# Linear attention: mask added in PSUM by TensorE, scores taken out half by ScalarE, half by VectorE; cross-attention clamp with a floor tile

## What is computed

```python
qp = relu(einsum('bhtd,hdm->bhtm', q_ch, proj))      # 64 features
kp = relu(einsum('bhtd,hdm->bhtm', k_ch, proj))
aw = einsum('bhtm,bhsm->bhts', qp, kp) * mask        # mask = tril(ones(128, 128))
out = (ctx_hist + aw @ v) / (norm_hist + aw.sum(-1) + 1e-6)
```

## Time and profile before

| | busy us | share of the span |
|---|---|---|
| TensorE matmul (PE) | 1311.8 | 89% |
| TensorE weight load (PEld) | 1113.5 | 76% |
| VectorE (DVE) | 911.7 | 62% |
| ScalarE (ACT) | 573.1 | 39% |
| GpSimd (POOL) | 795.9 | 54% |

### The profile page before, as it was taken

One profiled execution on the slowest core, in us unless ns is written; L12 is line 12 of the kernel. 1 busy time (PEld: TensorE's weight loads), 2 busy tenths in 40 slices (PEclk: granted clock), 3 DMA queues, 4 the chain that ended last, 5 costly groups with the idle time before them and its releaser, 6 DMA issues.

```text
span 1473.3 us, 23156 instructions
## 1 busy us (share of the span) xinstructions
PE 1311.8 (89%) x9073; PEld 1113.5 (76%) x9073; DVE 911.7 (62%) x1729; ACT 573.1 (39%) x1172; POOL 795.9 (54%) x761
## 2 busy tenths in 40 slices
PE   6998999999999999988899888987884699999980
PEld 6997788888888888866666666666653699999980
DVE  4656622632442262234687787777884699999966
ACT  3566311211121121124344444433342477777742
POOL 4444566666576576523232344535565347888831
PEclk9998999999999999999899999988885799999995
DMA  5101233233343233213324324235531755666605
GB/s 177 39 18 39 73 99 122 86 101 101 107 136 100 86 100 100 75 42 83 108 64 121 94 68 111 52 110 134 144 144 36 227 203 209 231 234 227 223 15 165
DMA packets 63101, 169.53 MB, mean 115 GB/s; under 512 B 11029, under 2 KB 30735, under 8 KB 55056
## 3 DMA queue, kind: packets, MB, share of 16 engines
q1 hardware_dynamic: 52432, 122.19, 27.8%
q0 software_dynamic: 10560, 45.86, 8.8%
HBM read 138.57 MB, written 33.38 MB: 117 GB/s over the span
## 4 chain that ended last, share of the span: by engine, by line
PE 71%; DVE 16%; ACT 3%; issue 3%; POOL 2%; DMA 2%; SPq 1%; ACTq 0%; POOLq 0%; DVEq 0%
PE bank L410 16%; PE bank L412 15%; PE bank L411 15%; PE bank L1297 9%; PE bank L418 4%; PE bank L1056 3%; PE bank L1137 3%; DVE topE L1809 3%; DVE shiftE L1816 3%; DVE topE L1811 1%; PE bank L1213 1%; ACT x_tok L458 1%; PE bank L1124 1%; PE bank L1192 1%; DVE x_tok L1977 1%
## 5 line engine op out<-in xcount | busy, mean ns | idle before, releaser
L1680 DVE CAST hid_hi<-bank 128x512 fp32r<-128x512 f32 x96 | 66.4, 691 | 252.1 <-ACT bank L1412 251.0
L552 POOL TENSOR_TENSOR wpiece_lo<-wraw,wpiece_hi 128x1024 fp32r<-128x1024 f32 x88 | 211.1, 2398 | 7.3
L410 PE MATMUL bank<-hid_hi,wpiece_lo 128*128 128x512 f32 x512 | 199.3, 389 | 0.0
L412 PE MATMUL bank<-hid_hi,wpiece_hi 128*128 128x512 f32 x512 | 199.2, 389 | 0.0
L411 PE MATMUL bank<-hid_lo,wpiece_hi 128*128 128x512 f32 x512 | 199.2, 389 | 0.0
L550 POOL TENSOR_SCALAR wpiece_hi<-wraw 128x1024 fp32r<-128x1024 f32 x88 | 94.1, 1069 | 154.7 <-PE bank L412 126.7
L1412 ACT ACTIVATE bank<-bank,ffn_scales 128x512 f32<-128x512 f32 x64 | 42.4, 662 | 301.5 <-PE bank L412 301.5
L1498 ACT ACTIVATE staging<-bank 128x512 f32<-128x512 f32 x128 | 70.0, 599 | 129.4 <-PE bank L1213 117.7
L412 PEld LDWEIGHTS bank<-hid_hi,wpiece_hi 128*128 128x128 f32 x512 | 96.1, 188 | 20.1
L410 PEld LDWEIGHTS bank<-hid_hi,wpiece_lo 128*128 128x128 f32 x512 | 96.1, 188 | 20.1
L411 PEld LDWEIGHTS bank<-hid_lo,wpiece_hi 128*128 128x128 f32 x512 | 96.1, 188 | 20.0
(11 more groups left out here) (342 smaller groups left out, 3696.9 us busy)
## 6 DMA issues: line engine op xcount, KB each, us to landing
wraw<-in_C_w SPq DMA_DIRECT2D x88, 512.0 KB, 3.6
w2raw<-in_F_w SPq DMA_DIRECT2D x8, 1152.0 KB, 7.2
w1raw<-in_F_w SPq DMA_DIRECT2D x8, 1028.0 KB, 7.4
split_qk<-qk_hi SPq DMA_DIRECT2D x64, 128.0 KB, 3.8
xt_lo<-split_qk SPq DMA_DIRECT2D x8, 1024.0 KB, 6.4
xt_hi<-split_qk SPq DMA_DIRECT2D x8, 1024.0 KB, 5.1
split_qk<-qk_lo SPq DMA_DIRECT2D x32, 128.0 KB
split_qk<-ctx_raw SPq DMA_DIRECT2D x32, 128.0 KB, 3.8
```

Source lines behind the costliest of these rows:

```text
L410: pe.e.matmul(o, sl, mh, start=start and i == 0, stop=False)
L412: made = pe.e.matmul(o, sh, mh, start=False, stop=stop and i == n - 1)
L552: pool.e.tensor_tensor(pair[1], raw, f(pair[0]), ALU.subtract).then_inc(done, 1)
```

## The change

TensorE: ahead of the score matmuls of a D pair, two matmuls (one for each head) of an identity with a tile of two copies of the transposed mask, 0 or -2**126, put the mask into the two diagonal blocks; the score matmuls then add to it (`start=False`). These operands are in the type float32r. `mask_d` now holds mask, mask and identity. The wait for `s_mask` goes ahead of it.

The step that takes scores out is then a maximum with 0: for QUAD step 1 on VectorE (`tensor_scalar` in the place of `tensor_tensor`), for QUAD step 2 on ScalarE (Relu).

The load of `mask_d` moves: it goes to `aw[0]`, once C's last result has been taken out, and GpSimd copies it from there to `mask_d` ahead of its D and E steps. The waits on `l_db` count one load less.

The clamp of E's maxima (L1811) becomes a `scalar_tensor_tensor` with the tile `floor_e` (-lim, filled once by GpSimd) in the place of the second constant.

```diff
+MASK_ON_ACT, MASK_ON_DVE = (2,), (1,)
@@ GpSimd
+            pool.e.memset(floor_e[:, :], -lim).then_inc(s_vone, 1)
+            pool.wait_ge(l_ffn, 48)
+            pool.e.tensor_scalar(mask_d[:, :], aw[0][:, 0, :], 1.0, 0.0, ALU.mult, ALU.add).then_inc(s_mask, 1)
             for name, step, args in DE:
@@ SyncE
-            load(mask_d[:, :], a["mask_d"], l_db)
             load(dbo[:, :], a["D_bo"], l_db)
             last = use["C", "y", B - 1]
             sp.wait_ge(last.drained, last.done)
+            load(aw[0][:, 0, :], a["mask_d"], l_ffn)
@@ TensorE, QUAD steps 1 and 2
                     pe.wait_ge(u.drained, u.turn)
+                    pe.wait_ge(s_mask, 1)
+                    for g in range(2):
+                        diagonals = u.ap[:, g * 512:(g + 1) * 512].rearrange("p (t s) -> p t s", t=TT)[:, :, 0:P]
+                        pe.e.matmul(diagonals, mask_d[:, 2 * P:3 * P], mask_d[:, 0:2 * P].rearrange("p (t s) -> p t s", t=TT),
+                                    start=True, stop=False, skip_group_check=True)
...
-                            made = pe.e.matmul(o, ft[rows, k, 1, t * P:(t + 1) * P], ft[rows, k, 0, t * P:S], start=True, stop=True)
+                            made = pe.e.matmul(o, ft[rows, k, 1, t * P:(t + 1) * P], ft[rows, k, 0, t * P:S], start=False, stop=True,
+                                               skip_group_check=True)
@@ ScalarE
+                elif name == "QUAD" and step in MASK_ON_ACT:
...
+                    act.e.activation(aw[n % 4][:, :, :], u.ap[:, :].rearrange("p (g s) -> p g s", g=2)[:, :, 0:3 * P],
+                                     ACT.Relu).then_inc(u.drained, 1)
@@ VectorE
-                elif name == "QUAD" and step in (1, 2):
+                elif name == "QUAD" and step in MASK_ON_DVE:
...
-                    dve.e.tensor_tensor(aw[n % 4][:, :, :], u.ap[:, :].rearrange("p (g s) -> p g s", g=2)[:, :, 0:3 * P],
-                                        mask_d[:, None, :].to_broadcast([P, 2, 3 * P]), ALU.mult).then_inc(u.drained, 1)
+                    dve.e.tensor_scalar(aw[n % 4][:, :, :], u.ap[:, :].rearrange("p (g s) -> p g s", g=2)[:, :, 0:3 * P],
+                                        0.0, None, ALU.max).then_inc(u.drained, 1)
...
-                    dve.mark(dve.e.tensor_scalar(top[:, :], top[:, :], lim, -lim, ALU.min, ALU.max))
+                    dve.mark(dve.e.scalar_tensor_tensor(out=top[:, :], in0=top[:, :], scalar=lim, in1=floor_e[:, :], op0=ALU.min,
+                                                        op1=ALU.max))
```

More of the change, by code:

```diff
@@ L329, in build @@
         xd = [sbp(f"xd_{n}", [P, KC, S], F32R) for n in ("hi", "lo")]
-        proj, mask_d = sbp("proj", [P, PAIRS, P]), sbp("mask_d", [P, 3 * P])
+        proj, mask_d = sbp("proj", [P, PAIRS, P]), sbp("mask_d", [P, 3 * P], F32R)
         dbv, dbo, dbias = sbp("dbv", [P, D]), sbp("dbo", [P, D]), sbp("dbias", [P, 2 * KC])
@@ L349, in build @@
         q_e, k_e = ([x[:, i, :].rearrange("p (j s) -> p j s", j=PAIRS) for i in range(2)] for x in (xt_hi, xt_lo))
-        top_e = ring(2, lambda i: sbp(f"topE{i}", [P, 2 * TT]))
+        top_e, floor_e = ring(2, lambda i: sbp(f"topE{i}", [P, 2 * TT])), sbp("floor_e", [P, 2 * TT])
         shift_e = ring(3, lambda i: sbp(f"shiftE{i}", [P, 2 * TT, S]))
@@ L361, in build @@
         lim = CLAMP / scale_e
-        l_db, l_eb = sem("l_db"), sem("l_eb")
+        l_db, l_eb, s_mask = sem("l_db"), sem("l_eb"), sem("d_mask")
         s_dwo, s_ew = sem("dwo"), sem("ew")
@@ L648, in pool_program @@
                 elif name == "XT":
-                    add_bias("D", *args, dbo, l_db, 80)
+                    add_bias("D", *args, dbo, l_db, 64)
                 elif name == "DFIN" and step == 1:
@@ L1118, in tensor_program @@
                         pe.wait_ge(use["D", k, b].drained, use["D", k, b].done)
-                    pe.wait_ge(l_db, 80)
+                    pe.wait_ge(l_db, 64)
                     pe.wait_ge(u.drained, u.turn)
@@ L1447, in scalar_program @@
                     u = use["D", "qk"[step], b]
-                    act.wait_ge(l_db, 80)
+                    act.wait_ge(l_db, 64)
                     act.wait_ge(u.filled, u.full)
@@ L1464, in scalar_program @@
                     act.e.activation(feat[n % 2][:, :, :, :].rearrange("p k w s -> p (k w s)"), u.ap[:, :], ACT.Relu).then_inc(u.drained, 1)
+                elif name == "QUAD" and step in MASK_ON_ACT:
+                    b, i = args
+                    n, u = 2 * (b * QUADS + i) + step - 1, use["D", "s", b, i, step - 1]
+                    act.wait_ge(u.filled, u.full)
+                    if n >= 4:
+                        old = use["D", "a", *divmod((n - 4) // 2, QUADS)]
+                        act.wait_ge(old.filled, old.full)
+                    act.e.activation(aw[n % 4][:, :, :], u.ap[:, :].rearrange("p (g s) -> p g s", g=2)[:, :, 0:3 * P],
+                                     ACT.Relu).then_inc(u.drained, 1)
                 elif name == "QUAD" and step == 3:
@@ L1781, in vector_program @@
                     b, = args
-                    dve.wait_ge(l_db, 80)
+                    dve.wait_ge(l_db, 64)
                     values("D", b, v_d, dbv, use["D", "a", b - 1, QUADS - 1] if b else None)
-                elif name == "QUAD" and step in (1, 2):
+                elif name == "QUAD" and step in MASK_ON_DVE:
                     b, i = args
@@ L1807, in vector_program @@
                     scores = u.ap[:, :].rearrange("p (m s) -> p m s", s=S)
+                    dve.wait_ge(s_vone, 4)
                     dve.wait_ge(u.filled, u.full)
@@ L2037 @@
         "mask_a": np.where(tri > 0, 0, MASKED).astype(np.float32),
-        "mask_d": np.concatenate([tri.T, np.ones((P, P), np.float32), tri.T], 1),
+        "mask_d": np.concatenate([np.where(tri.T > 0, 0, MASKED).astype(np.float32)] * 2 + [np.eye(P, dtype=np.float32)], 1),
         "iota8": np.broadcast_to(np.arange(NE, dtype=np.float32), (P, NE)),
```

## The result

The changed kernel takes 1495.83 us (median of four runs, 1493.75 to 1500.47), the kernel before beside it 1480.7: a ratio of 1.0101, 95% interval 1.0079 to 1.0124. That is 15.1 us slower; the forecast was 4.3 us slower, and 1495.83 lies just above its range.

A forecast was written before the change was run, and what follows sets the result against it. VectorE was taken to bound part of the rounds by E's scores, the chain passing through D's score matmuls. 13.7 - 2.9 - 7 + 0.5 = +4.3 us gave 1484.8 against 1480.49, range 1472 to 1495.

The forecast's parts named there:

- The pair, +13.7: Two mask matmuls on TensorE ahead of D's score steps: 0.29 us each on 47 of 64 steps, +13.7 us.
- the 0.4 that the prediction named as a sign of being wrong: The prediction called itself wrong if the mask pair on TensorE took over 0.4 us.
- The number on the path, 47 of 64: D's score steps on the chain: 43.6 us booked on L1137, at 0.92 us a step, make 47 of 64.
- The clamp, -7: VectorE's clamp of E's maxima: the new form waits for the first GpSimd instruction only, -7 us, bounds 0 and -14.7.
- rival (a): The clamp's waits for GpSimd stay whole in the new form: +11.3 us, 1492 to 1494; chance 0.18.
- Scores taken out, -2.9: D's score steps, half moved to ScalarE: only three pieces of VectorE's time on the chain are saved, -2.9 us.
- rival (c): The freed VectorE counts, E's reduce starting earlier in one round in four: -15.4 for -2.9, 1472.3 us; chance 0.12.
- The start of D, +0.5: The mask's later load and GpSimd's copy put first scores near 644.9 us, mostly in a gap: +0.5, bounds 0 and 1.6.
- The 7.2 us outside of the span: Added to the forecast span of 1477.6 us to give the forecast time of 1484.8.
- The granted clock (d), ±3: Between 710 and 1010 us, changed lower-clock stretches are worth up to 12 us, 3 either way allowed; no chance of its own.

The follow-up runs named there:

- e3: Changed kernel without the two mask matmuls of each score step, the mask left out of the computation: 1472.14 us, ratio 0.9955 to the kernel before.
- e12: Changed kernel with the pair issued, but the scores overwriting its result and VectorE masking all scores: 1498.97 us, ratio 1.014 to the kernel before.
- e2: Changed kernel with both score tiles taken out by VectorE, none by ScalarE: 1495.54 us, ratio 1.0105 to the kernel before.
- e10: Changed kernel with the causal mask left out and all 64 score steps taken out by VectorE: 1476.42 us, ratio 0.9997 to the kernel before.
- e1: Kernel before with the clamp's new form alone (scalar_tensor_tensor with the floor tile): 1477.94 us, ratio 0.9998 to the kernel before.
- e8: Kernel before with the clamp of E's maxima and the wait behind it left out: 1463.76 us, ratio 0.9894 to the kernel before.
- e17: Kernel before with the clamp as a reduce by minimum over the maxima and a constant beside them: 1467.31 us, ratio 0.9926 to the kernel before.
- e19: Changed kernel with the clamp as a reduce by minimum in the place of the new form: 1481.3 us, ratio 1.0016 to the kernel before.
- e11: Changed kernel with the pair only ahead of QUAD step 2, VectorE masking step 1 (32 pairs for 64): 1487.26 us, ratio 1.0071 to the kernel before.

## Why the prediction was wrong

The side was right and the size wrong: by the interval, the change costs 12 to 18 us where the sum had 4.3. In the forecast's own terms the runs give 21.6 for the pair, 0 for the clamp and -6.6 for the rest, together +15.0. The forecast had 13.7, -7 and -2.4. The miss of 10.7 is 7.9 + 7 - 4.2. That the side came out right is no merit of the balance, which was off by 7 us and more in each of its two large terms, both times the same way. Step by step:

**The pair, +13.7, was 21.6 us (e3; 21.1 by e12 and 16.0 by e2, both against e10).** This is one half of the miss, and the step that failed is the price of a pair. I took 0.29 between two readings of the earlier trace rows, 0.24 and 0.22 + 0.12 = 0.34; these rows show how such matmuls follow a group and each other, but not what lies between the last of them and the 64-row scores. The timeline gives 0.41 to 0.43, which is 0.22 + 0.21, above my dearest reading and over the 0.4 that the prediction named as a sign of being wrong. A second pair adds 0.24 to 0.25, which is what the earlier trace rows do price. So a pair is 0.24 of columns and some 0.18 at the two changes from one group to the next. The number on the path, 47 of 64 by the share of L1137 in the chain, held as far as the traces tell: the same work took 20.1 us longer, and 47 x 0.43 = 20.2.

**The clamp, -7, was nothing (e1).** This is the other half, and it is rival (a), to which I gave 0.18. The step that failed is that a form with two SBUF inputs waits for the first GpSimd instruction only, which I argued from L449 and L1607. The changed kernel at the place that answers to the earlier trace rows:

```profile
825.74 1.27 POOL L553 TENSOR_TENSOR ctx_lo<-ctx_raw,ctx_hi 96x512 fp32r<-96x512 f32 x1
826.64 1.77 DVE L1831 SCALAR_TENSOR_TENSOR topE<-topE,floor_e 128x4 f32<-128x4 f32 x1
826.96 1.43 POOL L633 TENSOR_TENSOR x_tok<-x_tok,dbo 128x256 f32<-128x256 f32 x2
828.36 1.05 POOL L674 TENSOR_SCALAR staging<-staging 128x1024 f32<-128x1024 f32 x1
828.45 1.22 DVE L1837 SCALAR_TENSOR_TENSOR shiftE<-bank,topE 128x1024 f32<-128x1024 f32 x1
```

It was issued 0.9 us into L553, waited past the end of that and over the two instructions of L633, and ended at 828.41 with the second of these (828.39), 1.4 us past the end of L553 at 827.01. The old form waited for L670 too, 2.79 us. The sum over 64 fell from 31.1 to 25.4 us, but that was worth nothing that the runs can tell (e1). The rule of the Trainium skill that the prediction weighed against this step, "SBUF — State Buffer", "Who interferes with whom", gave the term as 0, and the runs side with it. In one point they go beyond what the prediction took from it, that the loser is blocked for the whole instruction: here the wait went on over two further instructions. Two rows were too thin to go against the rule. Behind L449's instruction GpSimd had no other one of that kind ready; behind L1607's it had (L552, at 39.32), and L1607 ended at 39.51 without waiting for it. Why the clamp's form waits over several and L1607 didn't isn't shown. That the place was worth something I had right: the chain booked 14.7 us of waits and 6.3 of need, 21.0 together, against 15.7 measured with the clamp left out (e8), and 10.9 by a form that really doesn't wait (e17). With e17's clamp the forecast's sum would have been 13.7 - 2.9 - 10.9 + 0.5 = +0.4; measured is +2.4 (e19), the rest of the pair's price less what else is gained.

**Scores taken out, -2.9 (bounds 0 and -15.4).** In the changed kernel 0 (e2, within 5), without the pair -6.2 (e10 and e3, within 3). Without the pair, then, something of rival (c) is there, at less than half of its -15.4; whether the pair takes it away again is open. The durations were right: 0.951 us on VectorE, 0.812 on ScalarE, with 2.3 us of waiting for it in all.

**The start of D, +0.5.** The time of the first scores was right; what it cost wasn't measured by itself. The first scores stand at 644.67, behind GpSimd's copy; I had said 644.9:

```profile
643.61 0.51 POOL L644 TENSOR_SCALAR mask_d<-aw 128x384 fp32r<-128x384 f32 x1
...
644.26 0.47 PE L1140 MATMUL bank<-mask_d 128*128 128x256 f32 x2 [2.69 <-POOL mask_d L644]
644.67 1.62 PE L1146 MATMUL bank<-feat 64*128 64x256 f32 x8
```

**The 7.2 us outside of the span.** Wrong, without harm to the difference. In every profiled run here time less span is 1.8 to 1.9 us (1493.75 and 1491.9 after). The profiled execution of before was itself a quick one, of about 1475, and the rest is scatter: 21 runs of before in one comparison went from 1473.0 to 1483.6 us.

**The granted clock (d), ±3.** Over whole runs its mean was 0.938 before (21 runs) and 0.942 in the changed kernel (4 runs): by (1 - clock) x length the changed kernel loses 4 to 5 us less, the sign that I allowed for and somewhat more than the size. The largest piece of it in the profiled executions is just behind 710 us. First before, then after:

```profile
710.00:720.00 10.00, 9.58 (x70) 6.70 (x68) 8.15 (x14) 0.98 (x2) 1.72 (x3) 0.79 0.00 0
720.00:730.00 10.00, 9.10 (x61) 7.36 (x62) 7.50 (x10) 6.20 (x11) 4.54 (x5) 0.66 0.29 68
```

```profile
710.00:720.00 10.00, 7.98 (x69) 5.57 (x68) 5.68 (x10) 2.75 (x5) 0.00 (x0) 1.00 0.36 126
720.00:730.00 10.00, 7.89 (x57) 5.91 (x57) 9.22 (x16) 3.30 (x7) 3.95 (x5) 1.00 0.00 0
```

That is 5.5 us which the changed kernel doesn't lose there. The kernel without the pair (e3) has 0.82 and 0.66 in these 20 us, and this is where the 2.6 us of the feature marks came back. Ahead of it TensorE was busy 61.3 of 70 us between 640 and 710 in the changed kernel, 57.7 in e3 and 56.9 before.

But a pair is not shown to raise the clock over the whole. From the first features to the fourth router product both e3 and the changed kernel lose 11.9 us by it, and their means over whole runs are the same, 0.942. The kernels with all scores on VectorE lose 22.2 us without the pair (e10) and 23.9 and 20.5 with it (e2, e12), and before lost 17.1. In these single executions it is rather the split that goes with the higher clock, with the pair and without. Only the second and third pair go with a higher clock in every reading: over whole runs its mean was 0.942, 0.951 and 0.952 with one, two and three, so the second pair saves (0.951 - 0.942) x 1490 = 13 us of loss, the third about 1.

**What stays open.** A second pair is 64 x 0.24 = 15.4 us on TensorE, the clock gave back at most 13 of it, and the kernel ended 3.7 us earlier (the intervals of the two ratios overlap by half). A third cost 8.9 of its 15.4 (within 5). The profiled executions part this a little: from the first features to the fourth router product they take 369.4, 371.0 and 381.8 us with one, two and three pairs, and lose 11.9, 6.8 and 3.4 by the clock. Without the clock's share the second pair costs 6.7 us there and the third 14.2. So the clock alone doesn't make the second pair cheap; what does isn't shown. Why the first 32 pairs (e11) cost four times the second 32 isn't settled either; e11's six runs spread over 14.7 us, more than those of most kernels here, so the ratio of the two may be less than that.

## What to carry to other kernels

Price added matmuls by the whole step, with the change of kind on both sides of them: 0.22 + 0.21 us here, where rows of matmuls of one kind gave 0.12 for a follower. The number of steps on the path could be taken from the share of the line in the chain. Compare kernels over the same work, from one named instruction to another, not over the same stretch of time: a fixed stretch made the clock of E's end look higher than it was. And a change of the other engine's work in the same loop has to be tried with the first change in and out, since savings and costs need not add up. A tiny operation with long waits on a busy engine is the place to look: try it in each form that the engine has, for the form decides whether it waits, and leave it out once to learn what there is to win.

## What the runs showed of the hardware

- A small operation of VectorE waited for GpSimd as a two-constant operation (up to 2.79 us) and as one with two SBUF inputs (up to 1.77 us), over three or four GpSimd instructions in a row; as a reduce from SBUF it took 160 to 164 ns in all 64 cases, in each of three kernels.
- A pair of 256-column float32r matmuls ahead of a group of 64-row float32 matmuls puts that off by 0.41 to 0.43 us, the second pair by 0.24 to 0.25, the third by 0.24.
- With a second set of 64 such pairs the mean granted clock of whole runs went from 0.942 to 0.951, and the kernel was no slower (ratios 1.0101 and 1.0076). The first set did not raise it clearly: 0.942 without it (e3) and with it, and 0.937 and 0.940 with all scores on VectorE (e10, e12).
- A higher clock alone gained nothing where TensorE isn't the bound: 0.87 for 0.81 over the same work of E, in 131.0 us and 130.6.
- The time of a kernel goes with its mean clock from run to run: in most kernels here, runs whose mean clock was 0.001 lower took some 0.5 to 1.5 us longer. It isn't so for every run: one of e2 had 0.902, where its others had 0.938 to 0.949, and took 1491.43 us, less than the median of 1495.54.
